# Value product with the queries on the partitions, in a fused cross-attention and feed-forward layer

## What is computed

```python
n = layernorm(x)
ln = ln_affine(n)                                  # then rounded to fp8 values, per input scale
q, k, v = heads(fp8(ln) @ wq), heads(fp8(ln) @ wk), fp8(ln) @ wv
qx      = heads(fp8(ln) @ wqx)                     # heads() normalises every head of 128
kx, vx  = heads(ctx @ wkx), ctx @ wvx
core    = gqa(q, k, v)                             # 16 heads, keys from x
xout    = gqa(qx, kx, vx)                          # 16 heads, keys from ctx
cat     = fp8(concat([core, xout]) / proj_smooth)  # one factor for each of 4096 columns
x1      = x + tanh(g0) * (cat @ wproj.T) * scale
h       = int8-like(layernorm(x1)) @ ternary(w_gate_up)
out     = x1 + tanh(g1) * (int8-like(silu(a) * b) @ ternary(w_down))
```

## Time and profile before

| | |
|---|---|
| median of 3 runs | 2002.35 us |
| profiled execution | 2004.23 us |
| its span | 2002.4 us |
| TensorE busy | 1668.2 us (83%) |
| VectorE busy | 1746.9 us (87%) |
| ScalarE busy | 1188.1 us (59%) |
| GpSimd busy | 1017.8 us (51%) |
| granted TensorE clock, mean | 0.95 |
| first and last row maximum start at | 138.3 and 1642.2 us |

### The profile page before, as it was taken

The page is one execution under the profiler, slowest core; times in us unless marked ns, Lnnn a source line. Parts: engine busy times, 40 slices in busy tenths (PEclk is TensorE's granted clock), DMA queues, the critical chain, the costliest instruction groups (busy, mean ns, idle before and its releaser), DMA issues.

```text
span 2002.4 us, 35210 instructions
## 1 busy us (share of the span) xinstructions
PE 1668.2 (83%) x11147; PEld 1013.2 (51%) x11164; DVE 1746.9 (87%) x4062; ACT 1188.1 (59%) x2963; POOL 1017.8 (51%) x1327
## 2 busy tenths in 40 slices
PE   1467777768899998989999777999999958999996
PEld 0344444445566665556666444555566623444442
DVE  5769989999999989999999999999999955777774
ACT  2025556546788886778797656677777851222222
POOL 3476666666766665676665455555666521000000
PEclk7678999898999999999999999999999978999997
DMA  2236666767999998889999878899998797333200
GB/s 86 84 119 148 145 150 133 171 151 175 197 225 195 211 227 185 179 191 226 202 204 197 183 173 180 191 212 214 209 188 163 135 237 242 88 92 88 74 17 16
DMA packets 664285, 325.48 MB, mean 163 GB/s; under 512 B 551328, under 2 KB 594464, under 8 KB 663072
## 3 DMA queue, kind: packets, MB, share of 16 engines
q1 hardware_dynamic: 664096, 323.17, 71.6%
HBM read 140.61 MB, written 48.23 MB: 94 GB/s over the span
## 4 chain that ended last, share of the span: by engine, by line
DVE 50%; PE 27%; POOL 9%; issue 7%; DMA 3%; ACT 3%; SPq 0%; POOLq 0%; DVEq 0%; ACTq 0%
DVE pp L948 9%; DVE nmx L938 9%; PE psum L687 5%; PE psum L662 5%; PE psum L645 4%; PE psum L633 3%; PE psum L605 3%; PE psum L704 3%; DVE xh L921 3%; DVE wbt L826 2%; DMA pt<-pp 2%; PE psum L612 2%; POOL raw L1353 2%; DVE cc L962 2%; DVE ast L907 2%
## 5 line engine op out<-in xcount | busy, mean ns | idle before, releaser
L633 PE MATMUL psum<-qk 128*128 128x512 f16 x1536 | 427.7, 388 | 74.5 <-DVE pp L948 71.1
L605 PE MATMUL psum<-wbt,xqt 128*128 128x256 f16 (+1 forms) x4096 | 413.8, 251 | 53.6 <-DVE xh L921 39.7
L1236 ACT ACTIVATE psum<-psum,nmx 128x512 f32<-128x512 f32 x512 | 341.1, 666 | 143.6 <-DVE nmx L938 139.3
L605 PEld LDWEIGHTS psum<-wbt,xqt 128*128 128x128 f16 x4096 | 334.5, 100 | 167.3 <-DVE xh L921 45.2
L948 DVE SCALAR_TENSOR_TENSOR pp<-psum,prs,pp 128x512 f16<-128x512 f32 x512 | 377.8, 738 | 16.5 <-ACT pp L1247 16.5
L1247 ACT ACTIVATE pp<-psum,prs 128x512 f16<-128x512 f32 x512 | 351.2, 686 | 20.9 <-DMA pt<-pp 20.9
L938 DVE TENSOR_REDUCE nmx<-psum 128x1 f32<-128x512 f32 x512 | 342.8, 670 | 17.9 <-PE psum L633 17.2
L1242 ACT ACTIVATE prs<-psm 128x1 f32<-128x1 f32 x512 | 108.1, 211 | 258.7 <-DVE psm L943 257.3
L1429 POOL TENSOR_TENSOR qk<-y,qk 128x512 f16<-128x512 f32 x192 | 233.7, 1217 | 16.0
L633 PEld LDWEIGHTS psum<-qk 128*128 128x128 f16 x1536 | 142.8, 99 | 166.2 <-DVE pp L948 79.8
L645 PE MATMUL psum<-pt,vx 128*128 128x512 f16 x768 | 203.3, 389 | 24.5 <-ACT cy L1255 21.5
(11 more groups left out here) (169 smaller groups left out, 2801.6 us busy)
## 6 DMA issues: line engine op xcount, KB each, us to landing
wbt<-ws SPq DMA_DIRECT2D x192, 256.0 KB, 3.6
ws<-wbt SPq DMA_DIRECT2D x64, 256.0 KB, 3.9
catd<-cy SPq DMA_DIRECT2D x64, 256.0 KB, 3.3
raw<-in_wgu SPq DMA_DIRECT2D x64, 256.0 KB, 3.6
wbt<-catd SPq DMA_DIRECT2D x8, 2048.0 KB, 9.8
raw<-in_w SPq DMA_DIRECT2D x32, 384.0 KB, 3.8
pt<-pp SPq DMA_TRANSPOSE x512, 3.5
raw<-in_wp SPq DMA_DIRECT2D x32, 256.0 KB, 3.7
```

The costliest lines, as they stand in the source:

```text
L605: ins = e.matmul(bank[:, o0:o0 + c1 - c0], xv[:, v, kt * 512 + tt * 128:kt * 512 + (tt + 1) * 128], wb[i][:, h, kt, c0:c1], start=kt == 0 ...
L633: ins = e.matmul(SB(n), qk[i][:, jq, u, ss], qk[i][:, jk, w, :], start=k == 0, stop=k == 2)
L1236: e.activation(SB(n), SB(n), ACT.Exp, bias=nmx[:, k], accum_out=psm[:, k]).then_inc(s["exp"], 1)
```

## The change

The value product is turned round: the turned probabilities of 128 queries are the stationary operand and the value tile with its 128 columns is the moving one, so that the queries lie on the partitions of the result. The probabilities stay unnormalised (a constant scale 2^11), and the sums are applied at the eviction, which is on VectorE now and takes four instructions of 128 columns for each head: the factor of the row from `rin`, the factor of the column (`proj_smooth`) from a row that was spread over the partitions. `catd` is stored with the tokens as rows, and `load_cat` turns it with DMA transposes when the second part reads it. Scores have three PSUM banks and the shared ring has four. `lo` moves to the end of VectorE's slot and one slot earlier, `turn` one slot earlier, statistics, normalisation and `v_hi` one slot later. `group_factors` and the clip move to GpSimd. `wps` moves to the memory of the second part and is loaded in the last eight slots; the other late loads are cut into pieces and issued earlier. The ternary rounding is two comparisons.

The diff, cut to its core:

```diff
-PVLAG = 9
+PVLAG = 8
-OUT_AT = {"clip": 17, "field": 18, "step": 19, "add": 20, "sub": (21, 23), "store": 26}
+OUT_AT = {"clip": 16, "field": 17, "step": 18, "add": 19, "sub": (20, 21), "store": 23}
+CAT_AT, WG_AT, WP_AT, ROW_AT = (-38, -22), (-60, -18), -8, -4
...
-    return [hc] if 0 <= hc < NHC and t == 2 else []
+    return [hc] if 0 <= hc < NHC and t == 3 else []
...
-    bank = {use: 5 + i % 3 for i, use in enumerate(order)}
-    older = {use: order[i - 3] for i, use in enumerate(order) if i >= 3}
+    bank = {use: 4 + i % 4 for i, use in enumerate(order)}
+    older = {use: order[i - 4] for i, use in enumerate(order) if i >= 4}
...
-        SB = lambda n: psum[:, n % 4, :]
-        OB = psum[:, 4, :]
+        SB = lambda n: psum[:, n % 3, :]
+        OB = psum[:, 3, :]
...
-                e.dma_start(cat[u % 2][:], catd[b][:, :, h * 256:(h + 1) * 256]).then_inc(s[f"cat_ld{u % 2}"], 16)
+                e.dma_start_transpose(cat[u % 2][:, 8 * k:8 * k + 8, :], catd[r0:r0 + 256, 1024 * k:1024 * k + 1024]
+                                      ).then_inc(s[f"cat_ld{u % 2}"], 16)
+            def load_wp(c):
+                q.wait_ge("hd_tr", NIT * 6)
...
+                e.dma_start(wps[:, 4 * c:4 * c + 4, :], wpd[:, 4 * c:4 * c + 4, 0:512]).then_inc(s["wp_ld"], 16)
...
-                if 0 <= n - 3 < NSLOT:
-                    turn(n - 3)
+                if 0 <= n - 2 < NSLOT:
+                    turn(n - 2)
...
-                q.wait_ge("lo", n - 3)
+                q.wait_ge("lo", n - 2)
                 ss = slice(st * 128, (st + 1) * 128)
...
             def pv(hc, t):
...
                 if t == 0:
-                    for k in range(4):
-                        q.wait_ge(f"tr{k}", 16 * (hc + 1))
                     q.wait_ge("vx_lo", it * 4 + 4)
                     q.wait_ge("o_y", hc)
-                for k, (u, w) in enumerate(((0, 0), (0, 1), (1, 0))):
-                    ins = e.matmul(OB, v[:, t, u, :], src[:, w, t, :], start=t == 0 and k == 0, stop=t == 3 and k == 2)
+                q.wait_ge(f"tr{n % 4}", 16 * (n // 4 + 1))
+                src, v = pt_part(n), vv[it % 3]
+                for kt in range(4):
+                    for k, (u, w) in enumerate(((0, 0), (1, 0), (0, 1))):
+                        ins = e.matmul(OB[:, t * 128:(t + 1) * 128], src[:, 4 * w + kt, :], v[:, kt, u, att, :],
+                                       start=kt == 0 and k == 0, stop=kt == 3 and k == 2)
...
-            def recip(n):
-                k = slice(n % 8, n % 8 + 1)
-                q.wait_ge("exp", n + 1)
-                e.reciprocal(psm[:, k], psm[:, k]).then_inc(s["rc"], 1)
+            def recip(hc):
...
+                e.reciprocal(r, psm[:, hc % 2 * 4:hc % 2 * 4 + 4]).then_inc(s["rc"], 1)
+                q.wait_ge("rc", hc + 1)
+                e.tensor_scalar(r, r, f, None, ALU.mult).then_inc(s["rf"], 1)
+            def o_out(hc):
...
+                for t in range(4):
+                    ins = e.scalar_tensor_tensor(y[:, t, hc % 2, :], OB[:, t * 128:(t + 1) * 128],
+                                                 rin[:, hc % 4 * 4 + t:hc % 4 * 4 + t + 1], row[it % 2][:, k, :],
+                                                 ALU.mult, ALU.mult)
...
             def lo(n):
-                e.scalar_tensor_tensor(pp[k][:, 1, :], SB(n), prs[:, n % 8:n % 8 + 1], pp[k][:, 0, :],
+                e.scalar_tensor_tensor(pp[k][:, 1, :], SB(n), PSCALE, pp[k][:, 0, :],
...
-                    q.done(e.tensor_scalar(f, f, wsc[:, k:k + 1], MAGIC, ALU.mult, ALU.add))
-                    q.done(e.tensor_scalar(ob, f, MAGIC, 1.0, ALU.subtract, ALU.min))
-                    e.tensor_scalar(ob, ob, -1.0, None, ALU.max).then_inc(s["l_t2"], 1)
+                    q.done(e.tensor_scalar(ob, f, wsc[:, k - 4:k - 3], 1.0, ALU.is_lt, ALU.mult))
+                    e.scalar_tensor_tensor(ob, f, wsc[:, k:k + 1], ob, ALU.is_gt, ALU.subtract).then_inc(s["l_t2"], 1)
...
             for n in range(FIRST, PAST):
-                if 0 <= n - 1 < NSLOT:
-                    recip(n - 1)
                 if 0 <= n < NSLOT:
                     row_max(n)
-                if 0 <= n - 2 < NSLOT:
-                    lo(n - 2)
-                for it, tt, half in tiles_at(n - 2):
+                for it, tt, half in tiles_at(n - 3):
...
-                for it, tt, half in tiles_at(n - 1):
+                for it, tt, half in tiles_at(n - 2):
...
+                hc, t = divmod(n - 5, 4)
+                if t == 0 and 0 <= hc < NHC:
+                    recip(hc)
+                for hc in out_at(n):
+                    o_out(hc)
...
+                if 0 <= n - 1 < NSLOT:
+                    lo(n - 1)
...
-            def scale(n):
...
-            def o_out(hc):
...
...
+            def group_factors(it):
...
+            def out_clip(pair):
+                y = cy[pair % 3][:]
+                q.wait_ge("o_y", 2 * pair + 2)
+                e.tensor_scalar(y, y, 448.0, -448.0, ALU.min, ALU.max).then_inc(s["o_c"], 1)
```

More of the change, by code:

```diff
@@ L288, in flamingo @@
         qk = [a(f"qk{i}", [128, 6, 2, 512], F16) for i in range(2)]
[L289 to L290 removed]
+        vv = [a(f"vv{i}", [128, 4, 2, 2, 128], F16) for i in range(3)]
         pp = [a(f"pp{i}", [128, 2, 512], F16) for i in range(4)]
@@ L293, in flamingo @@
         nmx = a("nmx", [128, 8])
-        psm, prs = a("psm", [128, 8]), a("prs", [128, 8])
+        psm, rin = a("psm", [128, 8]), a("rin", [128, 16])
+        row = [a(f"row{i}", [128, 4, 128]) for i in range(2)]
         cc, xtmp = a("cc", [128, 1024], BF16), a("xtmp", [128, 1024], BF16)
@@ L1149, in dve_program @@
                         stats_b(it, tt)
-                for k, step in enumerate(("clip", "field", "step", "add")):
+                hc, t = divmod(n - 5, 4)
[3 more added lines that the diff above has]
+                    o_out(hc)
+                for k, step in enumerate(("field", "step", "add")):
                     for pair in pairs_at(n, OUT_AT[step]):
@@ L1163, in dve_program @@
                     kv_lo(it)
-                if j == FACTORS_AT and 0 < ph + 2 < NIT:
-                    group_factors(ph + 2)
                 for b, t in x_steps(n, "stats"):
@@ L1276, in act_program @@
                 if 0 <= n - 1 < NSLOT:
-                    scale(n - 1)
+                    hi(n - 1)
                 if 0 <= n < NSLOT:
                     exps(n)
-                if 0 <= n - 1 < NSLOT:
-                    hi(n - 1)
-                for hc in out_at(n):
-                    o_out(hc)
-                for it, tt, half in tiles_at(n - 1):
+                for it, tt, half in tiles_at(n - 2):
                     if half == 1:
@@ L1457, in pool_program @@
                 ctx_hi(0, kt)
+            group_factors(0)
             for n in range(FIRST, PAST):
-                for it, tt, half in tiles_at(n - 1):
+                for it, tt, half in tiles_at(n - 2):
                     if half == 0:
@@ L1466, in pool_program @@
                     head_lo(it, o)
+                ph, j = divmod(n, SLOTS)
+                if j == FACTORS_AT and 0 < ph + 2 < NIT:
+                    group_factors(ph + 2)
+                for pair in pairs_at(n, OUT_AT["clip"]):
+                    out_clip(pair)
                 for k in range(2):
```

195 lines of the change are left out of this document (100 added, 95 removed).

## The result

| | before | after |
|---|---|---|
| median | 2002.29 us (in the same comparison) | 2119.48 us (2118.64 to 2121.21) |
| ratio to before, 95% interval | | 1.0589 (1.0570 to 1.0607) |
| span of the profiled execution | 2002.4 us | 2117.4 us |
| first and last row maximum start at | 138.3, 1642.2 us | 131.1, 1755.4 us |

The sign of the forecast was right, the size was not: +117 us against +31 predicted, and above the end of the range at 2085. The loop between the first and the last row maximum grew by 120 us (1504 to 1624); what lies outside it shrank by 5.

A forecast was written before the change was run, and what follows sets the result against it. VectorE was taken to set the pace, TensorE close behind. Work +10, locks +15, ScalarE waits -15, new waits +29 and hand-over -8 gave +31 on 2004.2 us, so a median of 2033 us, range 1972 to 2085.

The forecast's parts named there:

- VectorE's work: VectorE's instructions in the attention loop: 161 us removed, 171 us added, net +10 us.
- the chain: group_factors, five tiny dependent VectorE instructions: moving it to GpSimd removes 1.8 us, 31 times, 56 us.
- delay from GpSimd: Locking between VectorE and GpSimd on their shared port: +15 us, ends -29 and +58.
- VectorE waits for TensorE: New loop waits from TensorE's shorter lead and the value product waiting for o_out: +29 us, ends 0 and +90.
- VectorE waits for ScalarE: ScalarE loses scaling and eviction, so VectorE waits less for it in the loop: -15 us, nothing to -35.
- both placements lose one collision and gain one: Reason for putting VectorE–GpSimd locking at +15 us, nearer to zero between its ends.
- +10 if the turned loads delay the probabilities' transposes: Worse end of the hand-over and DMA term, which was taken at -8 us.
- upper end of +90: Worst case of the new TensorE–VectorE waits: 0.7 us in each of 128 groups.
- The value matmuls, +12: TensorE's 12 matmuls of 128 columns replacing 3 of 512: +0.1 us a group, 12 us in all.
- rival 4: Each block's short value matmuls end with an exposed 0.16 us tail on TensorE: +38 us, 2071 us; chance 0.05.
- The hand-over, -8: Loads issued earlier and in pieces at the passage to the second part: -8 us, ends -15 and +10.
- rival 3: TensorE and VectorE wait for each other every group, 2094 us, or the lock's upper end, 2076; chance 0.19 for both.

The follow-up runs named there:

- e9: Changed kernel with only statistics, normalisation, power and v_hi back in the slots of before: 2154.0 us, ratio 1.0759.
- e14: Kernel before with only the banks changed, three for scores and four shared, lo in its old place: 2092.4 us, ratio 1.0444.
- e5: Changed kernel with the value product one slot later in its group: 2138.7 us, ratio 1.0663.
- e6: Changed kernel with four score banks, one value bank, three shared, and statistics, normalisation and v_hi in their old slots: 2153.7 us, ratio 1.0757.
- e13: Changed kernel with the edits of e6 and e5 together: 2066.8 us, ratio 1.0325.
- e3: Kernel before with only group_factors moved from VectorE to GpSimd: 1988.5 us, ratio 0.9928.
- e12: Kernel before with group_factors (in slot 6) and the clip moved to GpSimd: 1974.6 us, ratio 0.9860.
- e4: Changed kernel with each head's four evictions on ScalarE, the factor of the column left out: 2105.4 us, ratio 1.0507.
- e10: Kernel before with only the eviction of a head moved to VectorE, as one 512-column instruction: 2029.8 us, ratio 1.0137.

## Why the prediction was wrong

No single term carries the miss. The prediction's terms against the account of the profiled executions, us more than before (their spans differ by 115):

| term | predicted | measured |
|---|---|---|
| VectorE's work (+10, plus the 28 of the chain that are delay) | +38 | +58 |
| delay from GpSimd (+15, less the same 28) | -13 | +16 |
| VectorE waits for TensorE | +29 | +22 |
| VectorE waits for ScalarE | -15 | +4 |
| VectorE waits for raw weights (queue and DMA, put at nothing) | 0 | +21 |
| its other waits | 0 | -1 |
| outside the loop | -8 | -5 |
| sum | +31 | +115 |

**Delay from GpSimd: the largest miss, and the first step that failed.** The factor chain's delay went as predicted (-27). What was put at +15 beside it measured +43, not far from its upper end of +58. The step was "both placements lose one collision and gain one", and the places named were wrong. The prediction asked about `field` and the new product; `field` has 422 ns and the product 235 and 254 (two forms), both nearly free. What pays is `step`, +15, and the rounding (L1006, L1007; slots 312 to 438), +30, which the prediction did not ask about. The rule cited from the Trainium skill ("SBUF — State Buffer", section "SBUF: two separate sides") holds in the rows shown: `o_out` with one SBUF tensor is never held (325 to 351 ns), the SBUF-only `step` is held for as long as L1443 runs. Applied to the rows of the new order instead of to single operations it would have asked where each SBUF operation falls beside GpSimd's splits.

**Waits for ScalarE, -15, and for the raw weights, nothing: the second step.** In the loop VectorE waited 7.9 us for `hi` and 9.2 for the row sums; the second kind is gone, and the first is 21.5 us, most of it in the late slots where ScalarE waits for transposes (19.2 between 1600 and 1756 us; 7.9 in the same slots before). That is the "+10 if the turned loads delay the probabilities' transposes", named and not taken. The 21 us for raw weights come between slots 0 and 95, from loads that the prediction did not look at.

**Waits for TensorE, +29:** measured +22 (scores +35, projections -14), and in the 33 slots without jobs VectorE's idle time rose by 6 us where 7 were predicted. In size the term was right. How it was worked out, from TensorE's period of 10.3 us against VectorE's 11.0, is not shown to be right: slots are of unequal length (1.9 to 5.1 us, fifth to ninety-fifth percentile), and a lead is spent in single slots. Where the same kernel keeps the statistics in their old slots (e9) VectorE waits 116 us for TensorE, 85 more than before and near the upper end of +90; with half the lead (e14) it is 111. The new order avoids most of that and pays in delay.

**VectorE's work, net +10:** 20 us short (18 with the 2 us of `step`). `o_out` came to +129 against 132, `lo` to -29 against -31, the clip to -25 against -26, and the factor chain took 49 to 52 us off against 56. Reciprocal and product came to +6 against +2, the two comparisons to 0 as work against -3, and a row maximum is 10 ns longer, 5 us in all.

**The value matmuls, +12, and rival 4:** right. They come 58 ns apart in the stream of 24 shown above, and TensorE's busy time in 352 slots grew by 14 us. The Trainium skill's 81 ns ("TensorE: Matmul & The Clock Gate", section "Back-to-back issue gap") isn't what this trace shows, and an exposed tail isn't either: the projection behind the stream of 12 begins 0.16 us before the stream's end.

**The hand-over, -8:** behind the last row maximum the kernel takes 2 us more; the 5 us less outside the loop are a start that is 7 us shorter, for which the prediction had no term. The 7.5 us wait of the last `hi` is gone, but TensorE now waits 7.9 us there for the projection weights, which come from memory.

**Which rival.** None as it stands. Of rival 3 (0.19 for the two) the lock came near its upper end, which alone was put at 2076; mutual waits in every group (2094) did not come in the loop as changed. The other misses stood in no rival.

**How the 117 us divide.** Single edits on the kernel before give: three score banks with `lo` in its old place +91, eviction on VectorE +28, factors and clip on GpSimd -27, two comparisons +2 (within what can be told apart from nothing). Their sum is 94, but they are no shares of the 117: e14's lead is half that of the change, and e5, e6 and e13 show that the parts don't add up. The new slots of statistics and `lo`, the turned value product and the late loads were not isolated. From the other side, e13 gets back 53 and still stands 65 us above the kernel before. By the account that is 64 of work (of which 129 is `o_out`, less what was taken off), 42 of idle time, less 40 of delay. `lo` two slots behind its row maximum, as before, was not tried with the new value product.

## What to carry to other kernels

Work out the new order's collisions row by row: which operation of the engine that sets the pace starts while GpSimd is in one of its own. Here that alone was missed by 28 us. Look at a smaller lead between two engines slot by slot, not by mean periods: with VectorE busy for 97% of the time and TensorE for 90%, one score bank less with `lo` in its old place cost 4.4% (e14), although TensorE was still busy for less of the time than VectorE. Where an engine waits for two releases in one queue, the gain of removing one can show only when the other is gone too. And work taken off the engine that sets the pace is worth what its neighbours leave of it: here 14 us for 45 (e3), 27 for 69 (e12), 14 for 113 (e4).

## What the runs showed of the hardware

- An SBUF-only VectorE operation started 0.05 us behind a GpSimd operation of 1.15 us takes 1.39 us in place of 0.41. An operation on two numbers took 1.19 us beside a GpSimd operation of 1.15 us, though its record begins 0.02 us before that one (L807). Placing `step` where GpSimd waits made 64 of them 42 us shorter in sum (e13).
- Matmuls of 128 columns, each with its own weight load, keep 0.058 us in a stream of 24 (granted clock 0.99 in that stretch). With the product turned round TensorE's busy time in 352 slots was 1.5% higher (915 against 901 us).
- A 128x128 eviction with two factors takes 337 ns on VectorE, four of them 1.11 us; one instruction of 128x512 with one factor takes 738 ns (e10). ScalarE takes 374 ns for the 128x128 one (e4).
